# One kernel of an audio tower block: the first norm's rows turned by VectorE in blocks and a memory round trip, for batches 3 to 15

## The reference, cut to what matters

```python
h = gelu(x[:, 1:] @ W[:D] + x[:, :1] @ W[D:] + b)      # 16 x 374 x 256

def _layernorm(x, axis=-1, eps=1e-05):
    m = jnp.mean(x, axis=axis, keepdims=True)
    v = jnp.var(x, axis=axis, keepdims=True)
    return (x - m) / jnp.sqrt(v + eps)

def _L0_attn_ref(x):                                   # cosine attention on the first norm
    norms = jnp.linalg.norm(x, axis=-1)
    dots = jnp.einsum('bil,bjl->bij', x, x)
    sim = dots / jnp.maximum(norms[:, :, None] * norms[:, None, :], EPS)
    atten = jax.nn.softmax(sim, axis=-1)
    out = jnp.einsum('bij,bjl->bil', atten, x) + x
    return out

# _L0_ffn_ref on the second norm: a router picks experts per token (mask m, 8 experts),
q = jnp.einsum('tc,ecd,te->td', x, q_proj, m)          # k and v alike
scores = jnp.einsum('bqd,bkd->bqk', qh, kh) / jnp.sqrt(jnp.asarray(D, qh.dtype))   # causal
final = jnp.einsum('td,edc,te->tc', attn_out, o_proj, m * routing_weights)

h = h + _L0_attn_ref(_layernorm(h, axis=-1))
h = h + _L0_ffn_ref(_layernorm(h, axis=-1), ...)
```

## Time and profile before

| | |
|---|---|
| median of 3 runs | 713.16 us (713.08 to 713.31) |
| the profiled execution | 713.09 us |
| its span on the core | 711.4 us |
| TensorE busy | 704.6 us, 99% |
| VectorE busy | 581.6 us, 82% |
| ScalarE busy | 378.9 us, 53% |
| GpSimd busy | 399.6 us, 56% |
| granted TensorE clock | 1.0 |

### The profile page before, as it was taken

The page is one execution under the profiler, slowest core; times in us unless marked ns, Lnnn a source line. Parts: engine busy times, 40 slices in busy tenths (PEclk is TensorE's granted clock), DMA queues, the critical chain, the costliest instruction groups (busy, mean ns, idle before and its releaser), DMA issues.

```text
span 711.4 us, 18105 instructions
## 1 busy us (share of the span) xinstructions
PE 704.6 (99%) x5400; PEld 471.7 (66%) x5400; DVE 581.6 (82%) x1453; ACT 378.9 (53%) x807; POOL 399.6 (56%) x654
## 2 busy tenths in 40 slices
PE   8999999999999999999999999999999999999997
PEld 7888666675757666675756666575766667575655
DVE  6788798888879888888979888887988888886636
ACT  4977374554646464463646355463646455464443
POOL 7552325756465566746566575746566674643434
PEclk9999999999999999999999999999999999999999
DMA  9761220201020110102020020202011020201010
GB/s 234 171 178 46 69 48 9 72 3 63 14 63 14 22 55 0 70 7 63 14 56 22 11 66 0 70 7 63 14 32 46 0 70 7 63 17 53 15 75 30
DMA packets 33424, 34.35 MB, mean 48 GB/s; under 512 B 7282, under 2 KB 29170, under 8 KB 33266
## 3 DMA queue, kind: packets, MB, share of 16 engines
q1 hardware_dynamic: 32310, 33.36, 17.4%
q10 hardware_dynamic: 1084, 0.61, 0.3%
HBM read 27.70 MB, written 6.26 MB: 48 GB/s over the span
## 4 chain that ended last, share of the span: by engine, by line
PE 97%; DVE 1%; DMA 1%; ACT 0%; ACTq 0%; issue 0%; DVEq 0%
PE bank L1601 76%; PE bank L1664 7%; PE bank L1518 4%; PE bank L1575 3%; PE bank L1507 1%; PE bank L1735 1%; DMA gate_tmp<-in_L_ffn_gates_dram 1%; PE bank L1650 1%; PE bank L1523 1%; PE bank L1713 1%; PE bank L1686 0%; PE bank L1675 0%; PE bank L1678 0%; ACT xm L824 0%; PE bank L1776 0%
## 5 line engine op out<-in xcount | busy, mean ns | idle before, releaser
L1601 PE MATMUL bank<-xm,w_qkv 128*128 128x374 f16 x2304 | 415.7, 322 | 0.0
L1601 PEld LDWEIGHTS bank<-xm,w_qkv 128*128 128x128 f16 x2304 | 220.8, 98 | 139.2
L854 ACT ACTIVATE region_c<-bank,out_w 128x256 f32<-128x256 f32 x180 | 84.8, 471 | 163.2 <-PE bank L1601 162.2
L1206 DVE TENSOR_TENSOR xm<-xT,mask_all 128x1496 f16<-128x1496 f16 x128 | 152.0, 1209 | 0.0
L1601 PE MATMUL bank<-w_o,aoT 128*128 128x512 f16 x540 | 143.2, 379 | 0.0
L1118 DVE SCALAR_TENSOR_TENSOR h<-bank,out_w,h 128x256 f32 (+1 forms) x180 | 86.5, 480 | 49.0 <-ACT region_c L854 44.0
L626 POOL TENSOR_TENSOR region_c<-region_c 128x512 f32<-128x512 f32 x46 | 76.5, 1663 | 27.8 <-ACT region_c L854 23.1
L641 POOL TENSOR_TENSOR exp_hl<-exp,exp_hl 128x128 f16<-128x128 f32 (+2 forms) x48 | 41.8, 872 | 83.8 <-ACT exp_hl L810 83.4
L1601 PEld LDWEIGHTS bank<-w_o,aoT 128*128 128x128 f16 x540 | 50.4, 98 | 39.6
L1097 DVE TENSOR_SCALAR region_b<-h,moments,small 128x256 f32 (+1 forms) x96 | 48.8, 553 | 5.0 <-POOL small L547 5.0
L629 POOL TENSOR_TENSOR region_c<-region_c 128x256 f32<-128x256 f32 x46 | 47.9, 1041 | 8.2 <-POOL region_c L626 8.2
(11 more groups left out here) (193 smaller groups left out, 1063.1 us busy)
## 6 DMA issues: line engine op xcount, KB each, us to landing
mask_all<-d_mask SPq DMA_DIRECT2D x32, 384.0 KB, 3.8
h<-in_x_dram SPq DMA_DIRECT2D x16, 256.0 KB, 5.6
out_dram<-h SPq DMA_DIRECT2D x32, 128.0 KB
rnorm_row<-d_rnorm SPq DMA_DIRECT2D x16, 192.0 KB, 3.9
h<-in_x_dram SPq DMA_DIRECT2D x16, 112.0 KB, 6.2
out_dram<-h SPq DMA_DIRECT2D x16, 112.0 KB
xm<-in_L_ffn_q_proj_dram SPq DMA_DIRECT2D x2, 512.0 KB, 8.3
region_c<-in_L_ffn_k_proj_dram SPq DMA_DIRECT2D x2, 512.0 KB, 8.1
```

The costliest lines, as they stand in the source:

```text
L854: a.activation(prod[:, prod_buf(n, t), q, :], pair_bank(n, p)[:, C:2 * C], ACT.Copy, scale=weights_out(n)[:, t, 2 * q + 1:2 * q + 2]).then ...
L1206: v.tensor_tensor(xm[:, e, :, 0:T], xT[1][:, :, :, 0:T].rearrange("p a c t -> p (a c) t"), mask_all[:, e, 0:T].unsqueeze(1).broadcast_to([ ...
L1601: last = t_.matmul(dst, left[lp], right[rp], start=(starts and k == 0), stop=(stops and k == 2), skip_group_check=True)
```

## The change

For batches 3 to 15 the twelve transposes of `turn_first(g1)` are gone. In their place VectorE turns the float32 rows `xs[0]` in one instruction in blocks of 32 x 32 (`turn_blocks`), which leaves each block turned but in its old place; SyncE writes these blocks to memory in one DMA (`blocks_out`, 128 x 768 float32, 3072 bytes in each partition) and reads them back in four (`blocks_in`), each to 32 partitions, in runs of 32 float32 numbers, so that every block lands where it belongs (`xs_turned`, in the place of `xs[1]`). ScalarE rounds them to the high half of `xT[0]` (`turned_high`), and GpSimd takes the low half (`turned_low`). Batches 0 to 2 still go by TensorE.

With that the orders of work change: on VectorE `norm_apply(0, g1)` stands whole, with `turn_blocks`, right behind `pairs(2, 4)`, ahead of `weight_max` and pair 4; on ScalarE `high(0, g1)` stands ahead of pair 4, and `turned_high` between pairs 9 and 10; the copy `turned_probs_low(n)` goes from VectorE to ScalarE; on SyncE `blocks_out` stands between the two halves of `mask_around` and `blocks_in` behind them; on GpSimd `turned_low` stands between `low_1` and `add_tile(n, 1)`.

```diff
+        blocks = region_b[:, 2 * NT * C:3 * NT * C]
+        xs_turned = part(region_b, NT * C, NT, NC, P)
+        d_blocks = nc.dram_tensor("d_blocks", [P * NT * C], F32, kind="Internal").ap()
...
+            def blocks_out(g):
+                sp.wait_ge(s_blocks_turned, g - BY_BLOCKS + 1).then_inc(s_sp_passed, 1)
+                if after_blocks(g):
+                    sp.wait_ge(s_blocks_loaded, 16 * (P // SQ) * (g - BY_BLOCKS)).then_inc(s_sp_passed, 1)
+                sp.dma_start(d_blocks.rearrange("(p n) -> p n", p=P), blocks).then_inc(s_blocks_stored, 16)
+
+            def blocks_in(g):
+                sp.wait_ge(s_blocks_stored, 16 * (g - BY_BLOCKS + 1)).then_inc(s_sp_passed, 1)
+                sp.wait_ge(s_lo2, g).then_inc(s_sp_passed, 1)
+                columns = d_blocks.rearrange("(a i k b j) -> b i k a j", a=P // SQ, i=SQ, k=NT * NC, b=P // SQ)
+                for b in range(P // SQ):
+                    sp.dma_start(xs_turned[b * SQ:(b + 1) * SQ, :, :, :].rearrange("p t c (a j) -> p (t c) a j", a=P // SQ),
+                                 columns[b]).then_inc(s_blocks_loaded, 16)
...
                 if f is not None and not early(m):
-                    mask_around(f)
+                    mask_out(f)
+                    if g is not None:
+                        blocks_out(g)
+                    mask_in(f)
+                    if g is not None:
+                        blocks_in(g)
...
+            def turned_low(b):
+                pool.wait_ge(s_T1_hi, b + 1).then_inc(s_pool_passed, 1)
+                g.tensor_tensor(xT[0][:, 1, :, :].rearrange("p c (t w) -> p t c w", t=NT), xs_turned[:, :, :, :],
+                                xT[0][:, 0, :, :].rearrange("p c (t w) -> p t c w", t=NT),
+                                ALU.subtract).then_inc(s_T1_lo, 1)
...
                 if g1 is not None and not early(m):
                     low_1(g1)
+                    turned_low(g1)
...
+            def turned_high(b):
+                act.wait_ge(s_dots_done, NT * b)
+                act.wait_ge(s_blocks_loaded, 16 * (P // SQ) * (b - BY_BLOCKS + 1))
+                a.activation(xT[0][:, 0, :, :].rearrange("p c (t w) -> p t c w", t=NT), xs_turned[:, :, :, :],
+                             ACT.Copy).then_inc(s_T1_hi, 1)
...
                     turned_mask(f)
                     head_high(kT, qkv_bank[1], s_k_done, m + 1, s_k_hi, [(s_scores_done, NT * m)], qkv_out)
+                    if g1 is not None:
+                        high(0, g1)
                     scale_pairs(4, 5)
                     route_exp(f)
-                    scale_pairs(5, 7)
+                    scale_pairs(5, 10)
                     if g1 is not None:
-                        high(0, g1)
-                    scale_pairs(7, PAIRS)
-                    if g1 is not None:
-                        turned_rows(g1)
+                        turned_high(g1)
+                    scale_pairs(10, PAIRS)
                     high_v()
...
+            def turn_blocks(b):
+                dve.wait_ge(s_xs1, NT * (b + 1)).then_inc(s_dve_passed, 1)
+                if after_blocks(b):
+                    dve.wait_ge(s_blocks_stored, 16 * (b - BY_BLOCKS)).then_inc(s_dve_passed, 1)
+                v.transpose(blocks, xs[0][:, :, :].rearrange("p t c -> p (t c)")).then_inc(s_blocks_turned, 1)
...
                     residual(f)
-                    turned_probs_low(n)
...
                     pairs(2, 4)
+                    if g1 is not None:
+                        norm_apply(0, g1)
+                        turn_blocks(g1)
                     weight_max(f)
+                    pairs(4, 5)
                     head_low(kT, qkv_bank[1], s_k_hi, m + 1, s_k_lo, qkv_out)
-                    pairs(4, 5)
                     weight_sum(f)
...
-                    pe.wait_ge(s_T1_hi, f + 1)
+                    pe.wait_ge(s_logits_out, f)
                     turn_v(n)
...
                         pair(n, 5 + k)
-                    if g1 is not None:
-                        turn_first(g1)
                     M(23)
```

More of the change, by code:

```diff
@@ L226, in audio_tower_kernel @@
         s_T1_lo = sem("T1_lo")
+        s_blocks_turned = sem("blocks_turned")
+        s_blocks_stored = sem("blocks_stored")
+        s_blocks_loaded = sem("blocks_loaded")
         s_rn_stored = sem("rn_stored")
@@ L331, in audio_tower_kernel, with by_blocks, after_blocks @@
         RP = 8
+        SQ = 32
+        BY_BLOCKS = 3
+        def by_blocks(g):
+            return g is not None and not (isinstance(g, int) and g < BY_BLOCKS)
+        def after_blocks(g):
+            return not (isinstance(g, int) and g == BY_BLOCKS)
         def early(m):
@@ L453, in _ @@
             load_tiles(15)
-            mask_around(0)
+            mask_out(0)
+            mask_in(0)
             def store(n, t):
@@ L832, in turned_values, with turned_probs_low @@
                              as16(turn[0], 2 * NT * D), ACT.Copy).then_inc(s_v_tok_ready, 1)
+            def turned_probs_low(n):
+                if later(n):
+                    act.wait_ge(s_pv_done, n)
+                act.wait_ge(s_pT_lo_turned, n + 1)
+                a.activation(pT[:, 1, :], as16(turn[0], PW), ACT.Copy).then_inc(s_pT_lo, 1)
             def turned_probs(n):
@@ L883, in step @@
                         turned_values(n)
+                        turned_probs_low(n)
                         turned_probs(n)
@@ L1302, in output_weights, with last_probs_low @@
                 dve.wait_ge(s_out_w_ready, n + 1)
-            def turned_probs_low(n):
+            def last_probs_low(n):
                 dve.wait_ge(s_pT_lo_turned, n + 1)
-                if final(n):
-                    dve.wait_ge(s_pv_done, n)
+                dve.wait_ge(s_pv_done, n)
                 v.tensor_copy(pT[:, 1, :], as16(turn[0], PW)).then_inc(s_pT_lo, 1)
@@ L1370, in step @@
                     pairs(2, 4)
+                    if g1 is not None:
+                        norm_apply(0, g1)
+                        turn_blocks(g1)
                     weight_max(f)
+                    pairs(4, 5)
                     head_low(kT, qkv_bank[1], s_k_hi, m + 1, s_k_lo, qkv_out)
-                    pairs(4, 5)
                     weight_sum(f)
-                    if g1 is not None:
-                        norm_scaled(0, g1)
-                        norm_apply_tile(0, g1, 0)
-                    pairs(5, 6)
-                    if g1 is not None:
-                        norm_apply_tile(0, g1, 1)
-                        norm_apply_tile(0, g1, 2)
-                    pairs(6, 7)
-                    pairs(7, 8)
+                    pairs(5, 8)
                     for e in range(E - 3):
@@ L1422, in step @@
                 pairs(8, 9)
-                turned_probs_low(m)
+                last_probs_low(m)
                 last_values(m)
@@ L1645, in turn_exp @@
                 pe.wait_ge(s_exp1_lo, NT * f + NT - 1)
+                if by_blocks(f):
+                    pe.wait_ge(s_mask_row, f)
                 k = 0
```

3 lines of the change are left out of this document (2 added, 1 removed).

## The result

The changed kernel takes 749.24 us (median of 5 runs, 748.88 to 750.05) where the kernel before took 713.16: a ratio of 1.0508, with a 95% interval from 1.0497 to 1.0519. The forecast was 728.2 us, and slower; it is slower by 36.1 us where 15.1 were worked out. The profiled execution has a span of 747.2 us at the full granted clock.

A forecast was written before the change was run, and what follows sets the result against it. After the change TensorE and the VectorE chain were taken to be tied, with 0.13 us slack. Late pair 10 costs 1.16 us a step: 13 x 1.16 = 15.1 on 713.09, so 728.2 us, range 706 to 754 us.

The forecast's parts named there:

- What bounds the kernel: From pair 11 to `turn_exp`, TensorE's way (9.40 us) and the way through ScalarE and VectorE (9.27 us) are tied.
- Point 1: The transposes removed from TensorE: 0.66 us less a batch.
- Point 2: On VectorE, norm and block transpose (0.95 us) move ahead of pair 4; pair 6 on TensorE is a tie, cost 0.
- Points 3 and 4: Store, masks, then loads queue on the DMAs; 3072 runs of 128 bytes take 3.0 us; blocks land at 377.3.
- the third rival: Each 128 byte run is paid for by its write, 76 ns; blocks land at 388.9, 879 us; chance 0.07.
- Point 5: `turned_high` ahead of pair 10 on ScalarE makes pair 10's add 1.3 us late and `turn_exp` 1.16 us later.
- Point 6: GpSimd's `turned_low` ends at 379.8, wanted by `dots(f, 0)` at 379.90: cost 0; tile additions stay beside masks 3 and 4.
- Point 7: The low probabilities' copy moves into 3.12 us of ScalarE's waiting, cost 0; VectorE gets back 0.55 us.
- the slack of 0.13: The us by which TensorE's way from pair 11 to `turn_exp` exceeds the way through ScalarE and VectorE.
- my second rival: Blocks land at about 376.1 and only the slack is gained: 711.4 us at best, about 713, no change; chance 0.12.
- the first: Loads land in time and masks 3 and 4 are rid of GpSimd; all 0.66 us come out: 704.5 us; chance 0.24.
- the signs that I named: ScalarE waits over a microsecond before `turned_high`, VectorE before pair 10; TensorE idles 1.8 us a step; step about 41.7 us.

The follow-up runs named there:

- e5_two_turns: The kernel before with two of the twelve transposes of the first norm's rows left for batches 3 to 15: 713.07 us, ratio 0.9996.
- e11_short_tiles: e5_two_turns with GpSimd's additions for tiles 1 and 2 cut to 8 of 256 columns: 709.86 us.
- e10_short_low_late_norm: e8_late_norm with `turned_low` on GpSimd cut to 16 of 768 columns (8 of each half): 704.34 us.
- e8_late_norm: e2_landed with norm, `weight_max`, pair 4 and `kT` in the old order, block transpose behind pair 6, round trip behind the masks: 719.01 us.
- e3_between_masks: The changed kernel with the four loads of the blocks issued between the two mask loads: 734.66 us.
- e1_long_runs: The changed kernel with the blocks' loads bringing the same bytes in runs of 3072 bytes in place of 128: 744.33 us.
- e2_landed: The changed kernel with the full round trip still running but nobody waiting for it; `turned_high` and `turned_low` read `xs[0]`: 731.73 us.

## Why the prediction was off in size

**What bounds the kernel.** Right that TensorE is tied with another way, and that its 0.66 us were not to be had (`e5_two_turns`). Incomplete: there are two such ways. And the tie is no fixed length of VectorE's instructions. GpSimd's additions beside the masks make it: cut short, they leave VectorE's way 1.87 us shorter (`e11_short_tiles`), and what binds then is ScalarE's second copy. `e10_short_low_late_norm`, where the additions stand later and the copies behind pair 11 are gone, wins all 8.7 us.

**Point 1,** 0.66 us less on TensorE, right.

**Point 2,** the block transpose at 0.95 us: 0.98, with a wait of 0.34 more. Pair 6 came 0.17 us late on TensorE (386.01 - 16.49 = 369.52 for 369.35), a tie as said. What this point left out: `weight_max` stands behind the norm, and GpSimd's chain for the routing weights behind that. I followed VectorE's queue to pair 4 and not to the one who waits for `weight_max`. It put `low_1` under masks 0 and 1. In the changed kernel that hides behind the 1.41 us for which VectorE waits before pair 10; without the landing it is the larger part of the 18.4 us (`e8_late_norm`).

**Points 3 and 4,** the landing: 377.3 forecast, 378.03 measured (394.52 - 16.49). The store was issued at 369.18 (forecast 368.7) and the masks at 369.91 (369.0). Half of the masks' data out of the way brings the landing 1.14 us forward (`e3_between_masks`), runs of 3072 bytes 0.15 (`e1_long_runs`), so the queue, which the sum has, was the larger of the two. The price of a run was read wrongly: the digits of the earlier trace rows fill 17 slices, 1.28 us or 10 ns a run, and not 1.55 us and 12 ns. The straight line then gives 14 ns, a landing about 0.4 us earlier and a forecast about 5 us lower, further from the result.

The rule of the Trainium skill that I weighed ("DMA: Bandwidth & Descriptors", section Specifications: line rate needs at least 512 bytes) does not decide here: 3072 runs of 128 bytes a step cost the kernel 4.9 us more than long ones (2.8 to 7.0), against 151 us in the third rival.

**Point 5,** pair 10 behind `turned_high`, shown: scaled at 378.78 (forecast 378.1), added at 379.27 (378.65), that is 0.62 later than worked out.

**Point 6 is the step that failed.** It said that `turned_low` costs nothing, being in time for `dots(f, 0)` and hidden behind point 5, and that GpSimd's additions would stay beside masks 3 and 4. I asked when GpSimd is done and not what its work does to VectorE meanwhile, although the same point read off that two masks take 2.99 us beside the tiles. Each instruction of GpSimd that a mask meets puts its rest on VectorE's way, and the change adds one of 1.64 us: mask 2 meets `turned_low` and takes 1.81 us for 1.06. What the point said of `dots(f, 0)` did not hold either: `turned_low` ends at 380.69 in the clock of before, and TensorE waits 0.70 us for it, though the later waits for VectorE hide that. The 2.99 us were a wait for GpSimd too: masks 3 and 4 end at 382.12, 0.79 behind the tile's addition (379.37 + 1.96 = 381.33). I took them for a fixed price.

**Point 7,** cost 0 on ScalarE, no experiment speaks against it.

**The missed 1.59 us a step** (2.75 for 1.16) come together from the trace. Pair 10 is later by 0.62 and mask 2 longer by 0.75. Behind the cosines mask 5, which meets a tile's addition, takes 1.60 us for 1.45, so that the second `exp_low` ends 2.81 late (405.91 - 16.49 = 389.42 for 386.61), 0.14 more. And of the slack of 0.13 only 0.06 was there, since `turn_exp` starts 0.07 behind that end. That is 1.58. In the experiments the same two causes are not a sum. Without the landing 18.4 us stay, since the slowed masks alone make the way 1.4 us a step longer; with the landing they are partly in its shadow. So an early landing would not have brought the time back to 713 us with this order, as my second rival has it, nor to 704.5, as the first: with nobody waiting for the landing, `e2_landed` took 731.7.

The measured time lies in the stated range of 706 to 754 us, but that is luck. The upper part of the range stood for slow runs (26 ns, landing at 379.3), and the blocks landed at 378.0; what filled it was GpSimd's work beside the masks. Of the signs that I named, ScalarE's wait (2.38 us) and VectorE's before pair 10 came, and the step is 43.27 us and not 41.7.

Left open: how the landing splits into the store's completion, the issue time and the masks' packets, and why the long runs, with 1.25 us less of packets, land hardly earlier; and whether a kernel with the low half computed elsewhere, and the landing in time, would keep some of the 8.7 us. Neither was tried.

## What to carry to other kernels

When work is moved to an engine that is off the critical path, price it twice: once by when it ends, and once by what it does to the instructions of the engine beside it, with the durations that the trace has for these alone and in company. When an instruction is moved ahead in a queue, follow what it delays on to the other engines, and from there to what then runs side by side. Before believing in a gain from removed work, look for every way of the same length beside it: an experiment that only removes the work shows it in one run.
